# Two transposed score units per exponential in the first attention, and three subtractions moved one slot later

## The chip, the cores and the metric

The kernel runs on one core of one Trainium2 chip. The metric is device time in microseconds (us) of that core for one launch. Its engines run their own instruction lists in order and meet only at semaphores: TensorE (PE, with its weight loads PEld), VectorE (DVE), ScalarE (ACT), GpSimd (POOL) and SyncE (SP, which here only issues DMAs).

## The reference

Two transformer layers over x of 16 batches x 512 rows x 256 columns, each an attention with 16 heads of 16 columns and a feed-forward, all in float32. The change lies in the first attention:

```
qkv = layernorm(x) @ w_qkv + b_qkv
dot = einsum('bhid,bhjd->bhij', q, k)
scores = dot * dot / (|q_i|^2 + |k_j|^2 - 2 * dot + 1e-6)
attn = softmax(scores + causal_mask)
x = x + (attn @ v) @ w_out + b_out
```

## The kernel before

The program has four parts, one after the other: this attention (about the first 1,270 us of the profile), a low-rank feed-forward, a second attention and a second feed-forward. Only the first part is changed, in the function `ratio_attention`.

**Units and slots.** The first attention is cut into 640 units of 128 x 512 scores: 16 batches x 2 halves (8 heads each) x 20 units. Ten units make a group of four heads. A unit holds one block of 512 columns, one of 384 beside one of 128, or two of 256. Every engine walks through the same list of slots n, one unit entering per slot. What each engine does in slot n:

- PE: `dots(n)` (q times k into one of two banks), `turn(n - 6)` (four 128x128 transposes of finished scores into one of two banks, L554), `denoms(n + 3)` (the denominators), then, where the slot has it, preparation of the next half, and `attend` (probabilities times values, L220).
- ACT: `exponential(n - 6)` (L655: exp of the transposed unit, bank to SBUF), `inverse(n + 3)` (L644: Ln of the denominators; after every second one L648: Exp of two units together, 1/denominator), then preparation.
- DVE: `weigh(n)` (L789: dot times 1/denominator), `maxima(n)` (L799: times dot again, and the row maximum), then preparation.
- POOL: `less(n)` and `drop_later(n)` (L921, L930: maximum minus score, masked entries), then preparation.

**Preparation.** During the 20 slots of one half the next half's q, k, norms and values are made. The position in the half is what the texts call "slot 2", "slot 4" and so on (slot 20 is position 0 of the next half). From `PREP_AT`: q at 2, k at 4, the norms at 6, values at 9 and 12 or 13. For q and k: PE projects (L510), ACT stores the leading bf16 part and then the squares (L682, L684), DVE subtracts the leading part from the bank's value (L763, the "rest"), POOL splits the rest in two bf16 parts (L902, L904), SP sends the parts to DRAM and gathers them from there into the stacks that `dots` and `denoms` read. The norms go the same way (PE L520, ACT L691, DVE L769). Only the rest's semaphore, `prep_read`, gives the bank free.

**Banks.** PSUM has 8 banks: 2 for dots, 2 for the transposed scores, 1 for the outputs of `attend`, and 3 shared ones that `denoms`, the preparation and the output steps use in turn, so that each use waits until the use three before it has been read. The projection of k in slot 4 gets the bank of q's projection, and so waits for q's rest; the projection of q in slot 2 gets the bank of `denoms(4)` of slot 1, and so waits for the Ln of that unit.

**Waits that set the order.** `dots(n)` waits until `maxima` of unit n-2 is done; `weigh(n)` waits for `dots(n)` and the inverse; `turn(n)` waits for POOL's unit n and until `exponential(n - 2)` has emptied its bank. `denoms(n + 3)` for the next half begins in slot 17 and there waits until the half's DMA gathers have landed.

## Time and profile before

| | |
|---|---|
| median of 3 runs | 2637.72 us (2631.04 to 2639.08) |
| profiled execution: its own time, its span | 2632.14 us, 2630.4 us |
| mean granted TensorE clock | 0.987 of full speed |
| first to last `exponential` | 52.4 to 1268.4 us |
| 200 to 1200 us: PE, DVE, ACT, POOL busy | 947, 896, 923, 794 us |

The last row is the sum over five stretches of 200 us each. "Busy" is the share of time in which at least one instruction of an engine is in flight; the time between the starts of two neighbouring instructions is shorter than the duration of one, since they overlap.

### The profile page before, as it was taken

How to read it: one execution, taken by the hardware profiler on the slowest of the kernel's cores; microseconds unless marked ns; L12 is line 12 of the kernel's file. 1: busy time of each engine (PE TensorE's matmuls, PEld its weight loads, DVE VectorE, ACT ScalarE, POOL GpSimd, SP SyncE). 2: the span in 40 equal slices, each digit the busy share in tenths (PEclk: the TensorE clock that was granted, in tenths of full speed). 3: DMA queues.
4: the chain of work that ended last, by engine and by line, in shares of the span. 5: the costliest groups of instructions: out<-in, count | busy, mean ns of one | idle time of the engine just before them, and what ended most of it. 6: DMA issues, size and time to landing. Idle time of an engine off the chain costs nothing. (4 is left out here: it accounts for less than half of the span.)

```text
span 2630.4 us, 71983 instructions
## 1 busy us (share of the span) xinstructions
PE 2454.3 (93%) x25252; PEld 1750.0 (67%) x25252; DVE 2083.8 (79%) x6697; ACT 1996.4 (76%) x3679; POOL 1787.9 (68%) x3824
## 2 busy tenths in 40 slices
PE   5999999999999999999879989999999999989998
PEld 3677676667767666777423347767776777668887
DVE  5898898889889889988664578878888888846665
ACT  4999899999999999999524347677677666667776
POOL 4778778778877877887361137777777777756555
PEclk8999999999999999999989999999999999999999
DMA  4344244334334433433100146556655655400011
GB/s 119 65 74 81 55 73 85 72 61 83 72 58 79 85 71 61 77 69 63 37 6 1 37 74 111 99 101 98 106 101 95 105 104 94 64 1 32 25 33 41
DMA packets 110375, 182.00 MB, mean 69 GB/s; under 512 B 27008, under 2 KB 96384, under 8 KB 97920
## 3 DMA queue, kind: packets, MB, share of 16 engines
q1 hardware_dynamic: 106176, 175.82, 35.8%
q8 instruction: 203, 3.33, 0.6%
q10 hardware_dynamic: 3840, 1.58, 0.4%
q14 instruction: 156, 1.28, 0.2%
HBM read 116.25 MB, written 60.29 MB: 67 GB/s over the span
## 5 line engine op out<-in xcount | busy, mean ns | idle before, releaser
L921 POOL TENSOR_SCALAR ratio_scores<-ratio_scores,ratio_max_cols 128x512 f32<-128x512 f32 (+3 forms) x1024 | 539.3, 535 | 169.7 <-DVE ratio_max_cols L799 169.5
L205 PE MATMUL bank<-ratio_k_stack,ratio_q_stack 102*128 102x512 bf16 (+7 forms) x2048 | 508.7, 303 | 42.3 <-DVE ratio_max_cols L799 21.3
L1491 DVE CUSTOM_DVE_ANT_0 zeroed_unused<-bank,zeroed_drop 128x512 bf16<-128x512 f32 (+3 forms) x1024 | 439.7, 485 | 107.4 <-PE bank L205 107.2
L799 DVE CUSTOM_DVE_ANT_0 ratio_scores<-bank,ratio_scores 128x512 f32<-128x512 f32 (+3 forms) x1024 | 472.5, 490 | 22.2
L1373 ACT ACTIVATE arena<-bank 128x512 f32<-128x512 f32 x640 | 370.2, 593 | 151.0 <-PE bank L1266 149.6
L789 DVE TENSOR_TENSOR ratio_scores<-bank,ratio_inverse 128x512 f32<-128x512 f32 x640 | 435.6, 681 | 13.5 <-ACT ratio_inverse L648 6.5
L655 ACT ACTIVATE ratio_prob<-bank 128x512 f32<-128x512 f32 x640 | 378.6, 592 | 81.8 <-PE bank L554 80.9
L644 ACT ACTIVATE ratio_inverse<-bank 128x512 f32<-128x512 f32 x640 | 382.6, 598 | 13.4 <-PE bank L208 13.2
L554 PE MATMUL bank<-const_f_sb,ratio_scores 128*128 128x128 f32 x2560 | 386.5, 273 | 1.2 <-ACT ratio_prob L655 1.0
L648 ACT ACTIVATE ratio_inverse<-ratio_inverse 128x1024 f32<-128x1024 f32 x320 | 338.6, 1058 | 10.1
L1625 POOL TENSOR_SCALAR_AFFINE_SELECT arena<-arena 128x256 f32<-128x256 f32 (+1 forms) x640 | 228.0, 362 | 165.7 <-ACT arena L1373 161.2
L554 PEld LDWEIGHTS bank<-const_f_sb,ratio_scores 128*128 128x128 f32 x2560 | 296.0, 141 | 47.8 <-issue 11.0
L205 PEld LDWEIGHTS bank<-ratio_k_stack,ratio_q_stack 96*128 96x128 bf16 (+1 forms) x2048 | 178.0, 98 | 189.1 <-DVE ratio_max_cols L799 91.5
L930 POOL TENSOR_SCALAR_AFFINE_SELECT ratio_scores<-ratio_scores 128x256 f32<-128x256 f32 (+1 forms) x640 | 230.9, 361 | 47.0
L1266 PE MATMUL bank<-zeroed_q_stack,zeroed_k_stack 99*128 99x128 bf16 x2560 | 249.6, 219 | 11.7 <-ACT arena L1373 10.2
L205 PE MATMUL bank<-zeroed_k_stack,zeroed_q_stack 96*128 96x512 bf16 (+3 forms) x1024 | 247.3, 304 | 3.4 <-PEq L2161 2.1
L1266 PEld LDWEIGHTS bank<-zeroed_q_stack,zeroed_k_stack 99*128 99x128 bf16 x2560 | 178.1, 97 | 91.5 <-ACT arena L1373 55.1
L2414 POOL TENSOR_TENSOR ternary_square_sum<-ternary_square_sum,ternary_squares 128x512 f32<-128x512 f32 x112 | 144.6, 1291 | 121.2 <-ACT ternary_squares L2300 120.8
L208 PE MATMUL bank<-const_b_sb 128*128 128x128 bf16 x1024 | 193.2, 220 | 0.0
L1959 ACT ACTIVATE lowrank_hidden<-bank,lowrank_b 128x512 f32<-128x512 f32 x128 | 82.2, 685 | 132.9 <-PE bank L1841 132.8
L220 PE MATMUL bank<-ratio_prob,ratio_v_ones 128*32 128x128 f32 x5120 | 180.1, 277 | 0.0
L220 PE MATMUL bank<-arena,zeroed_v_ones 128*32 128x128 f32 x5120 | 179.4, 276 | 0.7
(218 smaller groups left out, 4872.0 us busy)
## 6 DMA issues: line engine op xcount, KB each, us to landing
ratio_q_stack<-ratio_parts_q SPq DMA_DIRECT2D x186, 128.0 KB
ratio_k_stack<-ratio_parts_k SPq DMA_DIRECT2D x186, 128.0 KB
zeroed_q_stack<-zeroed_parts_q SPq DMA_DIRECT2D x186, 128.0 KB, 4.5
zeroed_k_stack<-zeroed_parts_k SPq DMA_DIRECT2D x186, 128.0 KB, 7.5
ratio_parts_q<-arena SPq DMA_DIRECT2D x96, 128.0 KB
ratio_parts_k<-arena SPq DMA_DIRECT2D x96, 128.0 KB
zeroed_parts_q<-shared_parts SPq DMA_DIRECT2D x96, 128.0 KB
zeroed_parts_k<-shared_parts SPq DMA_DIRECT2D x96, 128.0 KB
```

What stands on the lines that cost most here:

```text
L205: i = e.matmul(bank[:, off:off + w], qs[0:rows, s, hh, ib * P:(ib + 1) * P], ks[0:rows, s, hh, 0:w], start=(k == 0), stop=mask is None, sk ...
L220: i = e.matmul(o_bank[32 * h:32 * h + 32, ib * P:(ib + 1) * P], values_ones[:, vs, jb, (g % 2) * GROUP + h, :], prob[:, (base + u) % bufs, ...
L554: i = e.transpose(bank[:, at:at + P], scores[:, n % S_BUFS, at:at + P], net.ident)
L644: e.activation(inv[:, n % INV_BUFS, :], shared("denoms", n)[:, :], ACT.Ln, scale=-2.0, bias=EPS_RATIO).then_inc(s["log_den"])
L648: e.activation(both, both, ACT.Exp, scale=-1.0).then_inc(s["inverse"])
L655: e.activation(prob[:, n % PROB_BUFS, 0:wd], exp_banks[n % 2][:, 0:wd], ACT.Exp, scale=-1.0).then_inc(s["prob"])
L789: e.tensor_tensor(scores[:, n % S_BUFS, 0:wd], dot_banks[n % 2][:, 0:wd], inv[:, n % INV_BUFS, 0:wd], ALU.mult).then_inc(s["weighed"])
L799: i = e.tensor_tensor_reduce(seg, dot_banks[n % 2][:, at], seg, 1.0, 0.0, ALU.mult, ALU.max, mx[:, pair % M_BUFS, c:c + 1])
L921: i = e.tensor_scalar(seg, seg, -1.0, mx[:, pair % M_BUFS, c:c + 1], ALU.mult, ALU.add)
L1266: i = e.matmul(bank[:, off + jb * P:off + (jb + 1) * P], ks[0:STACK + FOLD_ROWS, st, hh, jb * P:(jb + 1) * P], qs[0:STACK + FOLD_ROWS, st, ...
L1373: e.activation(prob[:, n % FOLD_PROBS, 0:wd], exp_banks[n % 2][:, 0:wd], ACT.Exp, scale=0.25).then_inc(s["prob"])
L1491: i = e.tensor_tensor_reduce(unused[:, n % 2, at], bank[:, at], drop[:, L - (ib + 1) * P:L], 1.0, 0.0, ALU.add, ALU.max, mx[:, pair % FOLD ...
```

## The change

Three edits:

1. The eight banks become one PSUM tensor of 128 x 8 x 512, so that one ACT instruction can read two neighbouring banks. In every odd slot ACT runs one `exponentials(p)` of 128 x 1024 over the two units n-7 and n-6, and none in even slots. The semaphore `prob` now counts pairs. Probabilities have 14 buffers instead of 13, scores 9 instead of 10.
2. PE transposes units n-7 and n-6 one after the other in odd slots, none in even slots. Both wait until the exponentials of the pair before have emptied both banks.
3. DVE's rests of q and k and of the norms (L763, L769) are issued one slot later, at 3, 5 and 7, behind that slot's `weigh` and `maxima`. PE's, ACT's and POOL's parts of the preparation stay in their slots.

```
-        self.banks = [ctx.enter_context(nc.psum_tensor(f"bank{i}", [P, 512], F32)) for i in range(8)]
+        self.psum = ctx.enter_context(nc.psum_tensor("bank", [P, 8, 512], F32))
+        self.banks = [self.psum[:, i, :] for i in range(8)]
...
-S_BUFS, INV_BUFS, PROB_BUFS = 10, 6, 13
+S_BUFS, INV_BUFS, PROB_BUFS = 9, 6, 14
...
             def turn(n):
...
-                q.wait_ge(s["prob"], n - 1)
+                q.wait_ge(s["prob"], n // 2)
...
-                if 0 <= n - BACK_LAG < total:
+                if 0 <= n - BACK_LAG < total and (n - BACK_LAG) % 2:
+                    turn(n - BACK_LAG - 1)
                     turn(n - BACK_LAG)
...
-                    q.wait_ge(s["prob"], g * N_UNITS + ATTEND_UNITS[part])
+                    q.wait_ge(s["prob"], (g * N_UNITS + ATTEND_UNITS[part] + 1) // 2)
...
-            def exponential(n):
-                wd = width(UNITS[n % N_UNITS])
-                q.wait_ge(s["turned"], n + 1)
-                if n >= PROB_BUFS:
-                    q.wait_ge(s["attended"], attended_by(n - PROB_BUFS))
-                e.activation(prob[:, n % PROB_BUFS, 0:wd], exp_banks[n % 2][:, 0:wd], ACT.Exp, scale=-1.0).then_inc(s["prob"])
+            def exponentials(p):
+                last = 2 * p + 1
+                q.wait_ge(s["turned"], last + 1)
+                if last >= PROB_BUFS:
+                    q.wait_ge(s["attended"], max(attended_by(last - 1 - PROB_BUFS), attended_by(last - PROB_BUFS)))
+                at = 2 * p % PROB_BUFS
+                e.activation(prob[:, at:at + 2, :], net.psum[:, EXP_BANK:EXP_BANK + 2, :], ACT.Exp, scale=-1.0).then_inc(s["prob"])
...
-                if 0 <= n - BACK_LAG < total:
-                    exponential(n - BACK_LAG)
+                if 0 <= n - BACK_LAG < total and (n - BACK_LAG) % 2:
+                    exponentials((n - BACK_LAG) // 2)
...
                 step = ratio_prep_at(n, halves)
-                if step:
+                if step and step[2][0] == "v":
+                    prepare(*step)
+                step = ratio_prep_at(n - 1, halves) if n else None
+                if step and step[2][0] != "v":
                     prepare(*step)
```

What stands in PE's list in slots 4 and 5 of a half (L510 the projection of k, L205 and L208 dots and denominators, L554 transposes, L220 attend), before:

```order
154 L205 MATMUL bank<-ratio_k_stack,ratio_q_stack 128x256 x2
155 L554 MATMUL bank<-const_f_sb,ratio_scores 128x128 x4
156 L205 MATMUL bank<-ratio_k_stack,ratio_q_stack 128x512
157 L208 MATMUL bank<-const_b_sb 128x128
158 L510 MATMUL bank<-arena,ratio_w_in 128x512 x2
159 L205 MATMUL bank<-ratio_k_stack,ratio_q_stack 128x512
160 L554 MATMUL bank<-const_f_sb,ratio_scores 128x128 x4
161 L205 MATMUL bank<-ratio_k_stack,ratio_q_stack 128x384
```

and after, where every line number is one or two higher:

```order
143 L206 MATMUL bank<-ratio_k_stack,ratio_q_stack 128x256 x2
144 L206 MATMUL bank<-ratio_k_stack,ratio_q_stack 128x512
145 L209 MATMUL bank<-const_b_sb 128x128
146 L512 MATMUL bank<-arena,ratio_w_in 128x512 x2
147 L206 MATMUL bank<-ratio_k_stack,ratio_q_stack 128x512
148 L556 MATMUL bank<-const_f_sb,ratio_scores 128x128 x8
149 L206 MATMUL bank<-ratio_k_stack,ratio_q_stack 128x384
```

The four transposes ahead of the projection are gone from slot 4, and eight stand together in slot 5.

DVE's list from `maxima` of slot 2 (the two L799 rows) to slot 5, before; L763 are the rests of q and k:

```order
120 L799 ISA ratio_scores,ratio_max_cols<-bank,ratio_scores 128x512
121 L799 ISA ratio_max_cols 128x1
122 L763 SCALAR_TENSOR_TENSOR arena<-bank,ratio_bias_qk,arena 128x512
123 L789 TENSOR_TENSOR ratio_scores<-bank,ratio_inverse 128x512
...
132 L799 ISA ratio_max_cols 128x1
133 L763 SCALAR_TENSOR_TENSOR arena<-bank,ratio_bias_qk,arena 128x512
134 L789 TENSOR_TENSOR ratio_scores<-bank,ratio_inverse 128x512
```

and after, with L767, L793 and L803 for the three:

```order
120 L803 ISA ratio_scores,ratio_max_cols<-bank,ratio_scores 128x512
121 L803 ISA ratio_max_cols 128x1
122 L793 TENSOR_TENSOR ratio_scores<-bank,ratio_inverse 128x512
...
126 L803 ISA ratio_max_cols 128x1
127 L767 SCALAR_TENSOR_TENSOR arena<-bank,ratio_bias_qk,arena 128x512
128 L793 TENSOR_TENSOR ratio_scores<-bank,ratio_inverse 128x512
```

The rest of q now stands behind slot 3's `weigh` and `maxima`, that of k behind slot 5's.

ACT's list around the end of a half (L655 exponential, L644 Ln, L648 Exp of two), before:

```order
115 L648 ACTIVATE ratio_inverse<-ratio_inverse 128x1024
116 L655 ACTIVATE ratio_prob<-bank 128x512
117 L644 ACTIVATE ratio_inverse<-bank 128x512
118 L655 ACTIVATE ratio_prob<-bank 128x512
119 L644 ACTIVATE ratio_inverse<-bank 128x512
120 L648 ACTIVATE ratio_inverse<-ratio_inverse 128x1024
```

and after (L659, L647, L651):

```order
87 L651 ACTIVATE ratio_inverse<-ratio_inverse 128x1024
88 L659 ACTIVATE ratio_prob<-bank 128x1024
89 L647 ACTIVATE ratio_inverse<-bank 128x512 x2
90 L651 ACTIVATE ratio_inverse<-ratio_inverse 128x1024
```

Of the two exponentials per pair of slots one is left, twice as wide, and it stands where the first one stood, ahead of the Ln of the odd slot.

## Rows read from the trace of the kernel before

**Rows 1.** Page, part 1: busy us, share of the span, instructions.

```profile
PE 2454.3 (93%) x25252; PEld 1750.0 (67%) x25252; DVE 2083.8 (79%) x6697; ACT 1996.4 (76%) x3679; POOL 1787.9 (68%) x3824
```

**Rows 2.** Waits, 200 to 1200 us: us in total, times, longest.

```profile
ACT ratio_prob L655 <- PE bank L554: 66.6, 90, 2.5
DVE arena L763 <- ACT arena L684: 62.1, 51, 2.6
...
DVE ratio_norm_rest L769 <- ACT ratio_n_parts L691: 10.1, 26, 0.6
...
DVE ratio_scores L789 <- PE bank L205: 4.1, 16, 0.8
```

**Rows 3.** Groups of PE, 200 to 1200 us: busy, mean ns | idle before, releasers.

```profile
L205 PE MATMUL bank<-ratio_k_stack,ratio_q_stack 96*128 96x128 bf16 (+5 forms) x1657 | 411.6, 302 | 25.3 <-DVE ratio_max_cols L799 13.7 <-DMA ratio_k_stack<-ratio_norms_k 10.3
...
L510 PE MATMUL bank<-arena,ratio_w_in 128*128 128x512 f32 x208 | 103.2, 618 | 21.8 <-ACT ratio_inverse L644 16.1 <-DVE arena L763 5.3
L532 PE MATMUL bank<-ratio_w_in,arena 128*128 128x128 f32 x416 | 58.2, 283 | 6.1 <-ACT ratio_inverse L644 6.1
```

**Rows 4.** Groups by shape, 400 to 720 us: busy, mean ns.

```profile
L655 ACT ACTIVATE ratio_prob<-bank 128x512 f32<-128x512 f32 x167 | 98.9, 592 | 21.4 <-PE bank L554 21.2
L648 ACT ACTIVATE ratio_inverse<-ratio_inverse 128x1024 f32<-128x1024 f32 x83 | 87.8, 1058 | 2.6
```

**Rows 5.** Timeline, slots 2 to 4 of a half: start, us, engine, line [idle before].

```profile
583.83 1.98 PE L510 MATMUL bank<-arena,ratio_w_in 128*128 128x512 f32 x4 [0.36 <-ACT ratio_inverse L644]
...
585.65 0.38 PE L205 MATMUL bank<-ratio_k_stack,ratio_q_stack 96*128 96x384 bf16 x2
...
585.87 0.60 PE L554 MATMUL bank<-const_f_sb,ratio_scores 128*128 128x128 f32 x4
...
586.31 0.33 PE L205 MATMUL bank<-ratio_k_stack,ratio_q_stack 102*128 102x384 bf16 x1
...
587.15 0.75 DVE L763 SCALAR_TENSOR_TENSOR arena<-bank,ratio_bias_qk,arena 128x512 f32<-128x512 f32 x1 [1.58 <-ACT arena L684]
...
587.82 0.68 DVE L789 TENSOR_TENSOR ratio_scores<-bank,ratio_inverse 128x512 f32<-128x512 f32 x1
...
587.95 1.98 PE L510 MATMUL bank<-arena,ratio_w_in 128*128 128x512 f32 x4 [0.20 <-DVE arena L763]
...
589.23 0.69 DVE L789 TENSOR_TENSOR ratio_scores<-bank,ratio_inverse 128x512 f32<-128x512 f32 x1
```

**Rows 6.** Timeline, slot 10 of the same half: dots(10) on PE, weigh(10) on DVE.

```profile
599.59 0.38 PE L205 MATMUL bank<-ratio_k_stack,ratio_q_stack 96*128 96x512 bf16 x1
...
600.60 0.68 DVE L789 TENSOR_TENSOR ratio_scores<-bank,ratio_inverse 128x512 f32<-128x512 f32 x1
```

**Rows 7.** Timeline, slots 20 to 22 behind an even half, up to the projection of q.

```profile
620.45 0.22 PE L208 MATMUL bank<-const_b_sb 128*128 128x128 bf16 x1
...
620.86 0.59 ACT L644 ACTIVATE ratio_inverse<-bank 128x512 f32<-128x512 f32 x1
...
621.48 1.06 ACT L648 ACTIVATE ratio_inverse<-ratio_inverse 128x1024 f32<-128x1024 f32 x1
...
622.44 0.58 ACT L672 ACTIVATE arena<-bank 128x512 f32<-128x512 f32 x1
...
622.92 0.59 ACT L655 ACTIVATE ratio_prob<-bank 128x512 f32<-128x512 f32 x1
...
623.40 0.60 ACT L644 ACTIVATE ratio_inverse<-bank 128x512 f32<-128x512 f32 x1
...
624.05 1.13 PE L510 MATMUL bank<-arena,ratio_w_in 128*128 128x512 f32 x2 [0.52 <-ACT ratio_inverse L644]
```

**Rows 8.** Timeline of PE and ACT, slots 20 and 21 behind an odd half.

```profile
657.66 0.39 PE L205 MATMUL bank<-ratio_k_stack,ratio_q_stack 96*128 96x384 bf16 x2 [0.25 <-DVE ratio_max_cols L799]
...
659.70 0.59 ACT L644 ACTIVATE ratio_inverse<-bank 128x512 f32<-128x512 f32 x1
...
660.35 1.12 PE L510 MATMUL bank<-arena,ratio_w_in 128*128 128x512 f32 x2
```

**Rows 9.** Timeline of PE and DVE, slots 17 and 18 of an odd half.

```profile
651.36 0.39 PE L205 MATMUL bank<-ratio_k_stack,ratio_q_stack 102*128 102x512 bf16 x1 [0.29 <-DMA ratio_k_stack<-ratio_norms_k]
...
652.75 0.39 PE L205 MATMUL bank<-ratio_k_stack,ratio_q_stack 96*128 96x384 bf16 x2
...
654.72 0.66 DVE L789 TENSOR_TENSOR ratio_scores<-bank,ratio_inverse 128x512 f32<-128x512 f32 x1
```

More of the change, by code:

```diff
@@ L306 @@
 SHARED = 3
+EXP_BANK = 3
 def ratio_prep(b, what):
@@ L460, in ratio_attention @@
         bk = net.banks
-        shared_banks, dot_banks, exp_banks, o_bank = (bk[0], bk[6], bk[7]), bk[1:3], bk[3:5], bk[5]
+        shared_banks, dot_banks, exp_banks, o_bank = (bk[0], bk[6], bk[7]), bk[1:3], bk[EXP_BANK:EXP_BANK + 2], bk[5]
         shared = lambda *use: shared_banks[use_at[use] % SHARED]
```

## The prediction

> **What bounds the kernel now.** I read the page first [rows 1]: PE 93%, DVE 79%, ACT 76%, POOL 68% over the whole program. That says little about one part, so I took the waits between 200 and 1200 us, deep inside the first attention; they cover 26 of its 32 halves. DVE there waits mostly for its own rests: 62.1 us at L763 for ACT's squares and 10.1 us at L769, together 2.8 us per half, and only 4.1 us for dots [rows 2]. ACT waits 66.6 us for transposes. Read alone, this says that DVE is the bound and that its 72 us are to be had. PE's groups over the same stretch speak against it: PE is idle only 25.3 + 21.8 + 6.1 = 53.2 us of 1000, or 2.05 us per half [rows 3]. PE, DVE and ACT are all near their limit and pass the limit on to each other. So I followed the timeline of one half and asked at each step which engine the others wait for. It falls into two stretches.
>
> From the projection of q (slot 2) to dots(10) PE sets the pace. In the half that begins at 583.83 this takes 599.59 - 583.83 = 15.76 us [rows 5, 6], and PE has one gap in it, 0.20 us ahead of k's projection, which waits for q's rest [rows 5]. DVE's waits of 1.58 us and so on lie inside this stretch, and DVE has caught up to one slot behind PE at its end: dots(10) ends at 599.97, weigh(10) starts at 600.60, 0.63 us later [rows 6]. From weigh(10) to the next projection of q DVE sets the pace first, and the last step is ACT's: q's projection waits for the Ln of slot 1, 16.1 us in 26 halves [rows 3].
>
> **Edit 1, ACT: one exponential of two units.** By durations, the wide one costs about what L648 costs, 1058 ns, against 2 x 592: 126 ns less per pair, 40 us of ACT over 320 pairs [rows 4]. But durations overlap. From start to start a 512-wide instruction takes 0.48 us (622.92 to 623.40) and the 1024-wide one 0.96 us (621.48 to 622.44) [rows 7], so two narrow ones cost exactly a wide one and the saving is 0. Bounds: 0 to 126 ns per pair; L648 reads SBUF where the new one reads a bank, so I take near 0, some 0.93 us for the new one from start to start. The Trainium skill ("Perfetto Trace Analysis", Optimizing Scalar/DVE Operations) gives ScalarE a fixed cost of about 51 ns per instruction on PSUM and 93 ns on SBUF, and says that grouping helps where the engine is saturated; by that the saving is an estimated 51 ns per pair, 16 us of ACT time over the kernel. ACT is no bound by itself (it waits 66.6 us for PE), so even 40 us would matter only where its Ln of slot 1 is awaited.
>
> What does move there is the order. Behind an even half ACT is late (it has stored x and kept a row): Ln 620.86, Exp of two 621.48, store of x 622.44, exponential 622.92, Ln 623.40 to 624.00, and PE projects q at 624.05 after 0.52 us idle [rows 7]. After the change the exponential of slot 20 no longer stands ahead, so the first Ln starts when its denominators end, 620.45 + 0.22 = 620.67, say 620.70. Then 0.62 + 0.96 + 0.48 as now gives 622.76, the wide exponential 0.93 more, 623.69, and the Ln 0.60: 624.29. That is **0.29 us later** per such half. Behind an odd half ACT is not late: dots(21) starts at 657.66 [rows 8], two turned units end 0.22 + 2 x 0.44 + 0.16 = 1.26 us later (the steps from dots to transposes and across one unit, 585.65, 585.87, 586.31, and a duration of 0.60) [rows 5], the wide exponential 0.93, the Ln 0.60: 660.45 against 659.70 + 0.59 = 660.29 now [rows 8]. **0.16 us later.** Two narrow exponentials could start after the first unit was turned; one wide one cannot.
>
> **Edit 2, PE: two units turned in odd slots.** PE's work is the same: 0.44 us per unit [rows 5]. I credit nothing for neighbouring transposes. Even slots give up 0.44 us and odd ones take it, so dots(n) of every even slot is issued 0.44 us later where PE is busy, and dots of odd slots as before. It matters where such a dots ends a PE stretch: slot 10. At slots 2, 4 and 6 it takes the transposes out of the slots that hold the projections. The gate from both banks is no wait by itself: the next pair comes two slots later, some 3.8 us, against about 1 us for the exponential. If that cover went, each pair would cost PE the rest of ACT's 0.93 us.
>
> **Edit 3, DVE: rests a slot later.** The wait for squares goes, but k's projection wants q's rest. dots(3) starts 585.65 and ends 586.03; weigh(3) and maxima(3) take 589.23 - 587.82 = 1.41 us, so 587.46; the rest takes 587.82 - 587.15 = 0.67, so 588.13; k's projection starts 0.05 behind it, about 588.20 instead of 587.95 [rows 5]. **0.25 us later**, where today DVE idles 1.58 us for nothing. From there PE is saturated, so dots(10) starts at 599.59 + 0.25 + 0.44 = 600.28 and ends 0.38 later, 600.66; weigh(10) follows at about 600.68 instead of 600.60 [rows 6]. So the 0.69 us fall almost wholly into the 0.63 us that DVE lags today: **0.08 us later** per half. The recovered waits show up as new waits of weigh for dots in slots 5, 6, 7, 8.
>
> POOL's split of q and k stands in its old slot and now waits for the later rest, with `less` of the next unit queued behind it; its results are wanted six slots on, and POOL is busy 68% [rows 1]. k's rest ends about 0.3 us later than now, since DVE arrives there later but does not wait. The gathers land for slot 17, where PE waits 10.3 us in 26 halves [rows 3]. In the odd half shown there the denoms start at 651.36, dots(18) at 652.75, and weigh(18) only at 654.72 [rows 9]: it ends at 653.14, 1.6 us of cover, and two turned units ahead of denoms fill 0.44 us of the wait. I price the DMA path at 0; without that cover it would be 0.3 us in 15 halves, 5 us. Score buffers 9 and probability buffers 14 put their waits behind events at least two slots old: 0.
>
> **Sum.** 31 halves prepare another. Per half with the late ACT 0.29 + 0.08 = 0.37 us, 15 times, 5.6 us; per other half 0.16 + 0.08 = 0.24 us, 16 times, 3.8 us. Together 9.4 us. The profiled execution took 2632.14 us, so 2641.5; it lies 5.6 us under the median of the three runs, and set against that median the forecast is 2637.7 + 9.4 = **2647 us**, 0.36% more. No change can be told from a change within 0.3%, 7.9 us. The likeliest case's own range is 3 to 15 us more, 2641 to 2653.
>
> **Rivals.**
>
> *The rests pay, faster.* If DVE's lag were the real limit at the end of each half, the 2.8 us per half that it waits would come back until PE's idle 2.05 us per half is used up: 31 x 2.05 = 63 us, 2575. Half of it is likelier, since the waits for DMA and for the Ln stay: 32 us, 2606. For it: PE's wait for maxima, 13.7 us [rows 3], and 0.25 us of it just ahead of q's projection [rows 8]. Against: the PE stretch of 15.76 us has no room. It decides if weigh(10) comes over 0.3 us earlier than 16.8 us behind the projection of q, which needs dots(10) to be early. Chance 0.27.
>
> *Nothing moves.* The wide exponential starts to start takes 0.86 us or less, ACT's lateness goes, and merging and shifting cancel within 3 us: 2638. For it: the slacks above are a tenth of a microsecond wide. This is also the case that the wide exponential saves only what the later start costs. Chance 0.14.
>
> *Dots late, and banks held, slower.* Between slots 14 and 20 of an even half PE is full too (output projections). If dots(16) and dots(18) each hold DVE 0.44 us and nothing takes it back, that is 0.88 us in each of 31 halves, 27 us: 2674 with the sum above. Against: in odd halves weigh(18) has 1.6 us of cover [rows 9], and behind even halves the chain through ACT is as long [rows 7]. The Trainium skill ("Perfetto Trace Analysis", Matmuls) wants matmul groups to rotate through PSUM banks so that the evacuation of one overlaps the next group; the change gives that up for the two transposed banks, and, under Optimizing Scalar/DVE Operations of the same page of the Trainium skill, instructions of an engine that isn't saturated are better broken up if they cause bubbles elsewhere. By these rules the time would come out on this side; no row here shows what that costs. It decides once ACT trails PE's odd slot by over two slots less 0.93 us. Chance 0.13.
>
> The forecast has 0.46, of which 0.26 beyond 7.9 us and 0.20 within. Faster: 0.25 (0.02 of that rival is too small to tell). Same: 0.20 + 0.14 + 0.02 = 0.36. Slower: 0.26 + 0.13 = 0.39. For the range I take in the upper half of the faster rival, down to 26 us less, and nearly all of the slower one: 2612 to 2672.
>
> **What would show each step.** Wide exponential: mean near 1.03 to 1.06 us and 0.93 from start to start; if 0.86, edit 1 gives more than I say. L767's wait for ACT gone; in its place about 0.5 us ahead of weigh in slots 5 to 8. Projection of q to projection of k: 4.37 us instead of 4.12. Projection of q to weigh(10): 16.85 instead of 16.77. PE's wait ahead of q's projection for the Ln grows from 0.62 us per half to 0.8. DMA waits in odd halves a little shorter. Two halves, from a projection of q to the second next: 77.1 us instead of 660.35 - 583.83 = 76.5 [rows 5, 8]. I am wrong if q's projection comes no later although the exponential is wide, if dots(10) has slack, or if PE waits for `prob` ahead of the pairs. The other three parts of the program should stay as they are to 1 us.

## The result and the profile after

The changed kernel takes 2660.07 us (median of 4 runs, 2659.28 to 2662.17) against 2637.09 (4 runs, 2631.04 to 2639.08): ratio 1.009, 95% interval 1.0073 to 1.0108. It is 23 us slower, 0.9%, where 0.36% was forecast. The profiled execution has a span of 2657.9 us.

The page of the changed kernel, part 1, and its group of the wide exponential (busy us, mean ns | idle before it):

```profile
PE 2453.8 (92%) x25252; PEld 1750.0 (66%) x25252; DVE 2091.2 (79%) x6697; ACT 1989.9 (75%) x3359; POOL 1789.7 (67%) x3824
...
L659 ACT ACTIVATE ratio_prob<-bank 128x1024 f32<-128x1024 f32 x320 | 325.4, 1017 | 23.3 <-PE bank L556 17.4
```

PE, nearest its limit, and ACT are busy no longer than before; DVE is, by 7.4 us, and POOL by 1.8 [rows 1]. The 23 us are mostly waiting. The waits of the changed kernel between 200 and 1200 us (total, times, longest; its L793, L767, L512, L534, L206, L647, L659 are L789, L763, L510, L532, L205, L644, L655 of before):

```profile
DVE ratio_scores L793 <- PE bank L206: 69.5, 116, 1.7
...
PE bank L512 <- ACT ratio_inverse L647: 22.2, 25, 1.5
PE bank L206 <- DVE ratio_max_cols L803: 17.5, 40, 0.7
...
PE bank L512 <- DVE arena L767: 14.1, 26, 0.5
PE bank L534 <- ACT ratio_inverse L647: 11.8, 13, 0.9
DVE ratio_v_ones L784 <- PE bank L534: 10.9, 26, 0.4
...
PE bank L206 <- DMA ratio_k_stack<-ratio_norms_k: 8.0, 9, 1.3
```

DVE no longer waits for ACT's squares (62.1 us [rows 2]); it waits 69.5 us for dots, where it waited 4.1. PE's own waits, the ones that count, add up to 73.6 us in the five rows of this view, against 51.5 in those of before [rows 3]: 6.1 more for the Ln ahead of q's projection, 8.8 more for q's rest ahead of k's projection, 5.7 more ahead of the values, 3.8 more for the maxima, 2.3 less for DMA.

The timeline of the half that begins at 588.96, from slot 2 to the values in slot 12:

```profile
588.96 1.98 PE L512 MATMUL bank<-arena,ratio_w_in 128*128 128x512 f32 x4 [0.78 <-ACT ratio_inverse L647]
...
591.20 0.69 DVE L793 TENSOR_TENSOR ratio_scores<-bank,ratio_inverse 128x512 f32<-128x512 f32 x1 [0.93 <-PE bank L206]
...
593.42 1.99 PE L512 MATMUL bank<-arena,ratio_w_in 128*128 128x512 f32 x4 [0.54 <-DVE arena L767]
...
602.34 0.69 DVE L793 TENSOR_TENSOR ratio_scores<-bank,ratio_inverse 128x512 f32<-128x512 f32 x1 [0.47 <-PE bank L206]
...
605.68 0.49 DVE L784 TENSOR_TENSOR ratio_v_ones<-bank,ratio_bias_v 128x128 f32<-128x128 f32 x2 [0.42 <-PE bank L534]
...
606.08 0.68 DVE L793 TENSOR_TENSOR ratio_scores<-bank,ratio_inverse 128x512 f32<-128x512 f32 x1
...
609.49 1.16 PE L534 MATMUL bank<-ratio_w_in,arena 128*128 128x128 f32 x8 [0.91 <-ACT ratio_inverse L647]
...
611.78 1.02 ACT L659 ACTIVATE ratio_prob<-bank 128x1024 f32<-128x1024 f32 x1 [0.77 <-PE bank L556]
...
612.70 0.59 ACT L647 ACTIVATE ratio_inverse<-bank 128x512 f32<-128x512 f32 x1
```

k's projection starts 593.42 - 588.96 = 4.46 us behind q's (before 4.12 [rows 5]), weigh(10) 606.08 - 588.96 = 17.12 us (before 16.77 [rows 5, 6]). DVE's last stop before it is new: the values step waits 0.42 us for PE. The wide exponential takes 612.70 - 611.78 = 0.92 us from start to start.

How much a period of two halves has grown is read from the first and the last projection of q behind an even half in the window, 12 periods apart. Before, then after:

```profile
235.44 1.98 PE L510 MATMUL bank<-arena,ratio_w_in 128*128 128x512 f32 x4 [0.52 <-ACT ratio_inverse L644]
...
1162.20 1.98 PE L510 MATMUL bank<-arena,ratio_w_in 128*128 128x512 f32 x4 [0.52 <-ACT ratio_inverse L644]
```

```profile
238.92 1.98 PE L512 MATMUL bank<-arena,ratio_w_in 128*128 128x512 f32 x4 [0.84 <-ACT ratio_inverse L647]
...
1179.64 1.99 PE L512 MATMUL bank<-arena,ratio_w_in 128*128 128x512 f32 x4 [0.84 <-ACT ratio_inverse L647]
```

(1162.20 - 235.44) / 12 = 77.23 us and (1179.64 - 238.92) / 12 = 78.39: 1.16 us more per two halves, 18.6 us over 16 of them. The profiled execution of before lost 1.8 of its 926.8 us in a stretch where the granted clock had fallen to 0.50 (last section); that of the changed kernel has no such stretch there, and with equal clocks the difference is 1.3 us per two halves. The end of the attention adds to it. There PE has little else to do and the gate from both banks, which costs nothing within the halves, is the limit. PE's last transposes in the changed kernel:

```profile
1284.84 1.06 PE L556 MATMUL bank<-const_f_sb,ratio_scores 128*128 128x128 f32 x8 [1.21 <-ACT ratio_prob L659]
1287.11 1.06 PE L556 MATMUL bank<-const_f_sb,ratio_scores 128*128 128x128 f32 x8 [0.77 <-ACT ratio_prob L659]
```

From the last weigh (1263.81 before, 1283.05 after) to the last attend (1270.33 and 1292.41) it is 2.8 us longer. With 0.7 us more up to the first weigh (40.52, 41.22) that makes 22.1 us by which the first attention ends later in the profile; the first weigh comes at 40.4 to 42.8 us in the profiles of all kernels here, so the 0.7 us can be chance. The code behind the first attention is the same in both kernels, and takes 1360.1 us in one profile and 1365.5 in the other (1360.1 to 1368.5 in the 14 profiles of this document). At one place in it the clock differs. The changed kernel, then before:

```profile
2345.00:2350.00 5.00, 4.10 (x11) 3.16 (x12) 0.16 (x1) 0.60 (x1) 0.00 (x0) 0.52 0.00 0
2350.00:2360.00 10.00, 6.06 (x15) 3.68 (x15) 4.11 (x13) 1.36 (x2) 0.76 (x3) 0.50 0.00 0
2360.00:2369.00 9.00, 7.48 (x20) 5.51 (x20) 4.41 (x10) 5.03 (x10) 3.91 (x8) 0.50 0.00 0
```

```profile
2333.00:2336.00 3.00, 2.60 (x6) 2.12 (x7) 2.95 (x8) 1.77 (x2) 2.99 (x9) 0.54 0.00 0
2336.00:2341.00 5.00, 3.28 (x15) 2.35 (x15) 2.18 (x5) 3.40 (x8) 1.70 (x3) 0.94 0.00 0
2341.00:2350.00 9.00, 7.71 (x51) 6.91 (x51) 5.50 (x9) 7.00 (x14) 5.18 (x4) 1.00 0.01 3
```

(The columns are the stretch, its length, busy us and instructions of PE, PEld, DVE, ACT and POOL, the granted clock as a share of 2.4 GHz, the DMA share and GB/s.) The granted clock is 0.50, 1.2 GHz, for some 24 us in the one and 3 us in the other. So the two profiles lie 27.5 us apart and the medians 23, and a difference of 4 or 5 us between medians need not come from the first attention.

### The profile page after: what moved, and what is told of

It is laid out like the page before. It is cut to its first block and busy times, and to the rows that moved or that the text cites. A ratio compares the mean times of both kernels' runs of the same rounds, so it can differ in the third digit from the quotient of the medians.

```text
span 2657.9 us, 71282 instructions
## 1 busy us (share of the span) xinstructions
PE 2453.8 (92%) x25252; PEld 1750.0 (66%) x25252; DVE 2091.2 (79%) x6697; ACT 1989.9 (75%) x3359; POOL 1789.7 (67%) x3824
## 3 DMA queue, kind: packets, MB, share of 16 engines
q14 instruction: 153, 1.25, 0.2%
## 5 line engine op out<-in xcount | busy, mean ns | idle before, releaser
L793 DVE TENSOR_TENSOR ratio_scores<-bank,ratio_inverse 128x512 f32<-128x512 f32 x640 | 437.0, 683 | 102.4 <-PE bank L206 88.8
L206 PE MATMUL bank<-ratio_k_stack,ratio_q_stack 102*128 102x512 bf16 (+7 forms) x2048 | 454.8, 303 | 42.5 <-DVE ratio_max_cols L803 26.5
L803 DVE CUSTOM_DVE_ANT_0 ratio_scores<-bank,ratio_scores 128x512 f32<-128x512 f32 (+3 forms) x1024 | 472.4, 489 | 22.0
L647 ACT ACTIVATE ratio_inverse<-bank 128x512 f32<-128x512 f32 x640 | 371.2, 599 | 80.4 <-PE bank L209 80.3
L651 ACT ACTIVATE ratio_inverse<-ratio_inverse 128x1024 f32<-128x1024 f32 x320 | 338.8, 1059 | 10.1
L659 ACT ACTIVATE ratio_prob<-bank 128x1024 f32<-128x1024 f32 x320 | 325.4, 1017 | 23.3 <-PE bank L556 17.4
L556 PE MATMUL bank<-const_f_sb,ratio_scores 128*128 128x128 f32 x2560 | 332.9, 273 | 4.3 <-ACT ratio_prob L659 4.0
L556 PEld LDWEIGHTS bank<-const_f_sb,ratio_scores 128*128 128x128 f32 x2560 | 287.4, 141 | 32.6 <-issue 13.1
L206 PEld LDWEIGHTS bank<-ratio_k_stack,ratio_q_stack 96*128 96x128 bf16 (+1 forms) x2048 | 178.8, 98 | 192.6 <-issue 81.5
L206 PE MATMUL bank<-zeroed_k_stack,zeroed_q_stack 96*128 96x512 bf16 (+3 forms) x1024 | 246.8, 303 | 3.8 <-PEq L2168 2.1
```

Of the source, the lines that this page charges most:

```text
L206: i = e.matmul(bank[:, off:off + w], qs[0:rows, s, hh, ib * P:(ib + 1) * P], ks[0:rows, s, hh, 0:w], start=(k == 0), stop=mask is None, sk ...
L556: i = e.transpose(bank[:, at:at + P], scores[:, n % S_BUFS, at:at + P], net.ident)
L647: e.activation(inv[:, n % INV_BUFS, :], shared("denoms", n)[:, :], ACT.Ln, scale=-2.0, bias=EPS_RATIO).then_inc(s["log_den"])
L651: e.activation(both, both, ACT.Exp, scale=-1.0).then_inc(s["inverse"])
L659: e.activation(prob[:, at:at + 2, :], net.psum[:, EXP_BANK:EXP_BANK + 2, :], ACT.Exp, scale=-1.0).then_inc(s["prob"])
L793: e.tensor_tensor(scores[:, n % S_BUFS, 0:wd], dot_banks[n % 2][:, 0:wd], inv[:, n % INV_BUFS, 0:wd], ALU.mult).then_inc(s["weighed"])
```

## The experiments

The table gives, from the timelines, means over 13 even and 13 odd halves between 200 and 1200 us, in us: from q's projection to k's; to weigh(10); from weigh(10) to weigh(20), even and odd; from there to the next projection of q, behind even and behind odd; two halves. Behind them the median and its ratio to before. Kernel before as timed beside them: 2637.3 (first four), 2636.6 (next four), 2635.9 (next three), 2637.9 (last). Three rows hold stretches at a granted clock of 0.50 in w10-w20 of odd halves, each behind a long wait of PE for DMA: one in before (1.8 us), two in e1 (4.5 us), five in e5 (12.4 us). The other odd halves take 16.7 us there in all three kernels, except one of 17.22 in e5 and the last, 15.2. Two such stretches lie in q-k of e10 (3.0 us).

```
                    q-k   q-w10  w10-w20 ev/odd  w20-q ev/odd  two halves  median   ratio (95%)
before              4.13  16.77  19.71 / 16.72   3.74 / 3.44   77.15
after               4.46  17.13  20.24 / 16.57   3.57 / 3.69   78.33       2660.1   1.0090 (1.0073-1.0108)
e1_rests_only       4.46  16.70  19.87 / 16.93   3.74 / 3.80   77.75       2647.5   1.0041 (1.0026-1.0056)
e2_pairs_only       4.12  16.79  20.25 / 16.61   3.57 / 3.67   77.67       2648.1   1.0041 (1.0025-1.0057)
e3_values_late      4.46  16.94  20.82 / 17.00   3.57 / 3.58   78.85       2666.4   1.0114 (1.0092-1.0136)
e4_two_narrow       4.46  17.13  20.19 / 16.57   3.63 / 3.52   78.17       2653.2   1.0060 (1.0043-1.0076)
e5_kn_late          4.13  16.37  19.87 / 17.57   3.74 / 3.75   77.67       2639.9   1.0012 (0.9999-1.0024)
e6_rows_even        4.5   17.2   19.52 / 16.57   4.77 / 3.63   78.86       2667.2   1.0107 (1.0092-1.0121)
e7_rests_x_later    4.46  16.70  19.87 / 16.61   3.74 / 3.32   76.95       2632.8   0.9987 (0.9975-0.9999)
e8_before_x_later   4.13  16.77  19.71 / 16.55   3.74 / 3.19   76.74       2629.0   0.9972 (0.9959-0.9985)
e9_kn_late_x_later  4.13  16.37  19.88 / 16.65   3.74 / 3.57   76.57       2627.5   0.9965 (0.9952-0.9978)
e10_rows_early      4.6   17.3   19.89 / 16.58   4.98 / 3.74   79.79       2675.0   1.0148 (1.0131-1.0164)
e11_after_x_later   4.46  17.13  20.24 / 16.57   3.58 / 3.28   77.93       2652.2   1.0060 (1.0044-1.0077)
e12_vb13            4.46  17.13  20.14 / 16.60   3.58 / 3.59   78.16       2656.2   1.0065 (1.0049-1.0081)
```

### e1 and e2: each edit alone

e1 is the kernel before with edit 3 alone; e2 has edits 1 and 2 and DVE's rests where they stood. The core of e1, DVE's loop:

```diff
-                if step:
+                if step and step[2][0] == "v":
+                    prepare(*step)
+                step = ratio_prep_at(n - 1, halves) if n else None
+                if step and step[2][0] != "v":
                     prepare(*step)
```

> The kernel before with edit 3 alone: DVE's rests of q, k and the norms one slot later, transposes and exponentials as before. Theory A (pairing costs, the rests don't): k's projection comes 0.25 to 0.33 us later, but DVE no longer lags at slot 10, so that projection of q to weigh(10) falls from 16.77 to about 16.5 us: 6 to 9 us less than before, 2629 us. Theory B (the later rest of q is what costs): 0.33 us in each of 31 halves, 10 us more than before, 2647 us.

> The changed kernel with DVE's rests back in their old slots: edits 1 and 2 alone. Theory A: most of the 23 us stays; projection of q to weigh(10) is 16.8 us as before, slot 15 of even halves keeps its 0.46 us and q's projection waits for the Ln as in the changed kernel: 13 to 18 us more than before, 2650 to 2655 us. Theory B: the pairs cost little, 10 to 13 us more at most, and k's projection is back at 4.13 us behind q's.

Each costs the same: 10.2 and 10.8 us, together 21 of the 23. So neither pays, and they add. In e1 weigh(10) comes 0.07 us earlier, although k's projection is 0.33 us late: the dots have slack as long as the transposes aren't moved. Its loss is behind weigh(10): 0.16 us in even halves, 0.36 ahead of q's projection behind odd halves, and 0.21 in w10-w20 of odd halves, which is the two stretches at a clock of 0.50. PE's waits in e1, 200 to 1200 us:

```profile
PE bank L205 <- DMA ratio_k_stack<-ratio_norms_k: 16.8, 12, 2.4
PE bank L510 <- DVE arena L763: 14.0, 26, 0.5
```

16.8 us for DMA against 10.3 [rows 3]; that path was priced at nothing. In e2 q to weigh(10) is as before, and the loss is the even half's last ten slots, 0.54 us, and the end of the attention, 2.8 us as in the changed kernel.

### e3 and e4: the values step, and the width

In e3 DVE's values steps too come a slot later than in the changed kernel, so that they don't wait behind the turned pair. In e4 the pair stays but gets two exponentials of 512, the first as soon as the first unit is turned:

```diff
-                q.wait_ge(s["turned"], last + 1)
...
-                e.activation(prob[:, at:at + 2, :], net.psum[:, EXP_BANK:EXP_BANK + 2, :], ACT.Exp, scale=-1.0).then_inc(s["prob"])
+                q.wait_ge(s["turned"], last)
+                e.activation(prob[:, at, :], exp_banks[0][:, :], ACT.Exp, scale=-1.0)
+                q.wait_ge(s["turned"], last + 1)
+                e.activation(prob[:, at + 1, :], exp_banks[1][:, :], ACT.Exp, scale=-1.0).then_inc(s["prob"])
```

> The changed kernel with DVE's step of the values one slot later too (slots 10 and 13 or 14), which the change left in place. The changed trace shows DVE idle 0.42 us there in each half, for PE's values. If that wait lies on the path between the projection of q and weigh(10), that stretch falls from 17.13 to 16.85 us and the kernel is 9 us faster than the changed one, 2651 us. If DVE is late for another reason (dots(10) itself), the wait moves to weigh(10) and the time stays at 2660 us.

> The changed kernel with two 128x512 exponentials in the odd slot instead of the wide one, each behind its own unit's transposes; all else as in the changed kernel. Theory: the wide one saves no time from start to start and can't start before the second unit is turned, so two narrow ones give 0.1 us per pair of halves and more back, 2 to 5 us less than the changed kernel, 2656 us. Rival: one instruction less is worth 0.05 to 0.13 us of ACT per pair ahead of q's projection, and the two narrow ones make it 5 us slower, 2665 us.

e3 splits what weigh(10) lost: 16.94 instead of 17.13, so 0.19 us were the values' wait; the other 0.17 are put down to the late dots(10). But the time rises by 6: behind weigh(10) even halves take 20.82 instead of 20.24 us and odd ones 17.00 instead of 16.57. The step had filled a gap of DVE, and now stands where DVE is full. My forecast missed by 15 us. e4 is 7 us faster than the changed kernel (2653.2 against 2660.1, intervals 1.0043 to 1.0076 and 1.0073 to 1.0108). The table shows 2.6 of them (16 x 0.16), most of it the Ln behind odd halves (3.69 to 3.52), and in its profile the last attend starts 2.8 us earlier (1289.64 against 1292.41) although its first weigh came 0.6 later (41.86). So some 3.4 us are the attention's. The other 4 us lie in the unchanged code behind it, which takes 1361.1 us in this profile against 1365.5, with the granted clock at 0.50 for some 10 us around 2350 instead of 24. The one execution of e4 with a mean clock of 0.983, where the changed kernel's four have 0.983 and 0.984, took 2656.1 us, 4 less than their median. The wide exponential saves nothing, and its later start costs a little.

### e5, e7 and e8: the rests apart, and the load of x

Before, SP issues the load of x (512 KB) right behind the last gather on which the next half's denoms wait. SP's issues in an odd half of before:

```profile
646.59 0.27 SPq L988 DMA_DIRECT2D ratio_k_stack<-ratio_norms_k  x1
646.91 0.40 SPq L1000 DMA_DIRECT2D x<-in_L_attn_x  x1
```

e5 shifts only the rests of k and the norms; e7 (on top of e1) and e8 (on top of before) issue x behind the next half's parts of q:

```diff
-                if m and b + 2 < B:
-                    e.dma_start(net.xb(b + 2), x_dram[b + 2].rearrange("(t p) d -> p t d", p=P)).then_inc(net.x_sems[(b + 2) % X_SEMS], 16)
                 sem = gathered(half)[0]
                 send_parts(half, 0)
+                if m and b + 2 < B:
+                    e.dma_start(net.xb(b + 2), x_dram[b + 2].rearrange("(t p) d -> p t d", p=P)).then_inc(net.x_sems[(b + 2) % X_SEMS], 16)
```

> The kernel before, with only the rests of k and of the norms a slot later; q's and the values' steps stay where they stood. My theory is that moving q's rest alone delays k's projection (4.13 us behind q's before, 4.46 with every rest late), while the steps of k and the norms lie in the stretch that PE sets. So: k's projection back to 4.13 us behind q's, weigh(10) 16.4 to 16.8 us behind q's projection, and 0 to 0.4 us per half less than before: 2625 to 2637 us. The rival is that k's later rest reaches PE by way of the gathers of the odd halves, where the run with all rests late waited 16.8 us for DMA against 10.3: then 3 to 7 us more than before, 2640 to 2644 us. The last group of gathers hangs on k's rest, so if the rival is right PE's wait for DMA between 200 and 1200 us is again above 14 us.

> The kernel before with all rests but the values' a slot later, as in the first experiment (2647.5 us), and in addition the load of x for two batches ahead issued behind the half's own parts, so that it does not share the queues with the gathers of the half before. Theory: the cost of the late rests in the odd halves (PE's wait for DMA 16.8 us between 200 and 1200 us, before 10.3) is a transfer that lands late, and this takes away what it competes with: the wait under 6 us, and 2638 to 2643 us. Rival: the wait is the late issue of the gathers themselves, or only the place where DVE's and PE's lateness shows: 2647 us, with the wait at 16 us as there.

> The kernel before with the load of x issued behind the half's own parts, and nothing else. If the 10.3 us that PE waits for DMA between 200 and 1200 us (11 instances of about 0.9 us, in odd halves) come from the load of x, up to 13 us over the 32 halves go: 2626 to 2634 us. If that wait is hidden or is made by the gathers alone: 2637 us, as before.

e5 confirms both the theory and its rival: weigh(10) gains 0.40 us in every half, the best of all, and the odd halves give it back, where PE waits 19.3 us for DMA in slot 17. What such a wait costs is seen half by half. In odd halves of before, PE's wait in slot 17 and the time from weigh(20) to q's projection, in us:

```
wait           0.29  0.54  0.85  1.09  1.25  1.51
weigh(20)-q    2.83  3.07  3.38  3.62  3.79  4.05
```

With no wait it is 2.79. So nearly the whole wait reaches q's projection, by way of the later denominators and their Ln; beyond some 1.5 us weigh(18) is late too (a half of e5 with a wait of 2.06 us: 17.22 us from weigh(10) to weigh(20) instead of 16.69). Most of the 0.85 us that slots 17 and 18 lose in the table is something else. Five odd halves, behind waits of 1.79 to 2.57 us, take 18.5 to 20.4 us, and in each the granted clock falls to 0.50 right behind the wait, as in this one:

```profile
723.33 0.39 PE L205 MATMUL bank<-ratio_k_stack,ratio_q_stack 102*128 102x512 bf16 x1 [2.43 <-DMA ratio_k_stack<-ratio_norms_k]
...
723.70 1.93 PE L220 MATMUL bank<-ratio_prob,ratio_v_ones 128*32 128x128 f32 x32
```

```profile
720.00:721.00 1.00, 0.89 (x8) 0.57 (x5) 0.96 (x6) 1.00 (x3) 0.93 (x3) 1.00 1.02 117
721.00:723.00 2.00, 0.00 (x0) 0.00 (x0) 1.93 (x7) 1.64 (x3) 0.79 (x2) 1.00 0.99 192
723.00:724.00 1.00, 0.67 (x10) 0.40 (x14) 1.00 (x4) 0.19 (x1) 0.93 (x4) 0.86 0.21 71
724.00:726.00 2.00, 2.00 (x35) 1.34 (x28) 0.58 (x4) 0.41 (x1) 0.82 (x2) 0.50 0.00 0
726.00:727.00 1.00, 1.00 (x7) 0.91 (x6) 0.75 (x2) 0.00 (x0) 0.00 (x0) 0.50 0.00 0
727.00:728.00 1.00, 1.00 (x22) 0.55 (x19) 0.71 (x4) 0.93 (x2) 0.18 (x1) 0.93 0.00 0
```

The five halves are 12.4 us longer together. If the waits cost there what they did at 2.06 us, an estimate from these rows is under 4 us for the waits and over 8 for the clock. How many such stretches the other executions of e5 had is not known; its median is only 3.3 us above before, where the table's 16 x 0.52 would give 8.3.

e8 is faster than before, by 7.6 us (0.9972, 0.9959 to 0.9985), from one moved DMA. The load is issued 20.5 us behind that gather (645.13, 665.63) instead of 0.3. PE's wait for DMA is 5.4 us (before 10.3), no wait in slot 17 is above 1.33 us, and the load lands in 4.6 us instead of 6.4; its line in the DMA issues of before and of e8, 200 to 1200 us:

```profile
x<-in_L_attn_x SPq DMA_DIRECT2D x11, 512.0 KB, 6.4
```

```profile
x<-in_L_attn_x SPq DMA_DIRECT2D x12, 512.0 KB, 4.6
```

Of the 0.41 us per two halves between the two in the table, 0.14 is the stretch at a clock of 0.50 in the profile of before. e7 takes 14.7 us from e1, more than forecast, though PE's wait for DMA is 8.8 us and not under 6. Without the load in the way the late rests cost 3.7 us (2632.8 against 2629.0) and not 10: two thirds of e1's loss are gathers that were issued later and met the load of x, with what the clock then took.

### e9: both gains together

> The kernel before with the rests of k and of the norms a slot later (alone 2639.9 us) and the load of x issued behind the half's own parts (alone 2629.0). In the first of the two, weigh(10) came 16.37 us behind q's projection instead of 16.77 in every half, and slots 17 and 18 of the odd halves gave it back, where PE waited 19.3 us for DMA. Theory: that is the gather in which the load of x shares the queues, and with it moved the gain stays. Even halves then 40.0 us from q to q, odd ones 16.37 + 16.6 + 3.3 = 36.3, together 76.3 against 77.15, 16 times 0.85: 14 us less than before, 2619 to 2627 us, with PE's wait for DMA under 10 us. Rival: the gathers end late for k's own later rest, and the two do not add: 2629 to 2636 us, with the wait still at 12 us or more.

2627.5 us, 8 less than before: the fastest, but not to be told from e8 alone (0.9965, 0.9952 to 0.9978, against 0.9972). The two don't add as hoped. weigh(10) keeps its 0.40 us and slots 17 and 18 lose only 0.1 (16.65 against 16.55), but the next projection of q behind odd halves comes 0.38 us later (3.57 against 3.19). PE still waits 12.5 us for DMA where e8 has 5.4, and by the rows above such a wait ends as one for the Ln. Its waits:

```profile
PE bank L510 <- ACT ratio_inverse L644: 17.8, 23, 1.4
...
PE bank L205 <- DMA ratio_k_stack<-ratio_norms_k: 12.5, 12, 1.8
```

### e11: how much of the changed kernel's loss is DMA

The changed kernel with e7's edit of SP.

> The changed kernel with the load of x issued behind the half's own parts. How much of its 23 us is the DMA path. It waits 8.0 us for DMA between 200 and 1200 us. Theory: its pairs hide part of the late gathers (the wait is less than the 16.8 us with the rests alone), so less is to be had than the 14.7 us which the same edit gave there: 3 to 8 us less than the changed kernel, 2652 to 2657 us. Rival: the cost of the late rests in it is the same DMA wait as without the pairs, then 12 us or more come back, 2645 to 2648.

8 us less, at the edge of the theory's range. Against e8, which has x moved too, it is 23 us slower, as the changed kernel is against before. So within the full change the load of x explains none of the 23 us, although it explains most of what the rests cost alone: the pairs leave the gathers time to land, and take it elsewhere.

### e6, e10 and e12: the even half's last ten slots

Three attempts on the 0.53 us there, each one number in the changed kernel's tables:

```diff
-RATIO_GROUP, RATIO_ROW = BACK_LAG + N_UNITS + 5, (53, 55, 57, 59)
+RATIO_GROUP, RATIO_ROW = BACK_LAG + N_UNITS + 5, (54, 56, 58, 60)      e6
+RATIO_GROUP, RATIO_ROW = BACK_LAG + N_UNITS + 5, (52, 54, 56, 58)      e10
-PREP_AT = ({2: "q", 4: "k", 6: "n", 9: "va", 12: "vb", 16: "x0"},
+PREP_AT = ({2: "q", 4: "k", 6: "n", 9: "va", 13: "vb", 16: "x0"},      e12
```

> The changed kernel, with the steps of the output rows of even halves one slot later, so that they fall in slots without pair transposes. My theory puts about 0.5 us of each even half's loss on slots 13 to 15, where a pair of turned units and a row's projection meet in one slot: then weigh(10) to weigh(20) in even halves falls from 20.24 to about 19.8 us, and the time to 2652 us (16 x 0.5 = 8 us less). The rival is that the place of the rows does not matter, because the pair's own 0.88 us in the odd slot holds DVE there: 20.2 us as now, and 2658 to 2662 us.

> The changed kernel, with the steps of the output rows one slot earlier than in it (slots 12, 14, 16, 18 of even halves instead of 13, 15, 17, 19), again away from the pairs. One slot later, weigh(10) to weigh(20) of even halves fell from 20.24 to 19.52 us, but the fourth step came into slot 0 of the next half and cost 1.5 us there. Theory: the pair and the row's projection in one slot cost the even half about 0.5 us, and with all four steps inside it and apart from the pairs it gets them back: 19.5 to 19.8 us in even halves, odd ones as now, 2650 to 2654 us. Rival: the loss only moves to the slots where the row now stands (dots of even slots ordered behind a row's turn), 20.2 us and 2658 to 2662.

> The changed kernel with the second values step of even halves in slot 13 instead of 12 (where it stands in odd halves). In even halves PE waits for a shared bank ahead of that step until ACT has read a denominator out of it, 11.8 us in 13 even halves between 200 and 1200 us against 6.1 before, 0.44 us more per even half, and weigh(10) to weigh(20) there has grown by 0.53. Theory: this wait is most of the even half's loss, since PE is full up to slot 20 there; one slot later the bank is free, the wait is gone (11.8 us to under 2), weigh(10) to weigh(20) falls from 20.24 to 19.6 to 19.9 us, and the time by 6 to 10 us, to 2650 to 2654. Rival: PE's work is only put into a slot that already holds a pair of turned units and a row's turn, the wait comes up elsewhere and the time stays, 2658 to 2662.

e6 and e10 shorten weigh(10) to weigh(20), by 0.72 and 0.35 us. For e6 that proves nothing, since its fourth step, 0.69 us of DVE behind a wait of 0.71, only went over into the next half. In e10 all four stay inside, so 0.35 us is a gain, and 1.4 us are lost at the border (4.98 against 3.57). There a new wait appears: 8.3 us in 13 halves for ACT's copy of the turned x, which holds one of the three shared banks. The rotation of these banks goes by order, and a moved step hands everybody another bank. e12 takes the wait ahead of the values away (L534 no longer shows in PE's waits). In its place the wait for the maxima is 5.8 us longer (17.5 in the changed kernel) and a new one for the Ln appears:

```profile
PE bank L206 <- DVE ratio_max_cols L803: 23.3, 54, 0.7
...
PE bank L206 <- ACT ratio_inverse L647: 3.7, 13, 0.3
```

The even half gains 0.10 us of the 0.53, the time 4 us (below the rival's range, above the theory's); by the table it is 2.7, and in the profile the last attend comes no earlier (1292.56 against 1292.41), so those 4 us aren't shown to be the attention's. The wait for a shared bank is where the loss shows, and mostly not its cause. With the pairs it is there in e2 too (11.8 us, 6.7 in e1), so it is the pairs that make it; which of their effects, the late dots of even slots or ACT's order, no run separates.

## Why the prediction was right, and where its sizes were off

The time lies in the range, 2612 to 2672, and on the side that had the largest chance, 0.39 against 0.36 and 0.25. It doesn't lie in the likeliest case's own range, 2641 to 2653: the wide one held it because it also covered the rivals. The sum said 9.4 us, 23 were measured, and the trace shows 22 (16 x 1.16, 2.8 and 0.7).

- **Wide exponential, 0.93 us from start to start:** 0.92. Right, and that it gives nothing is shown by e4, whose attention is 3.4 us shorter without it.
- **The Ln ahead of q's projection, 0.62 us per half growing to 0.8:** 22.2 / 26 = 0.85. Right. Over both halves the part behind weigh(10) was forecast at 0.29 + 0.16 = 0.45 us and measured 0.46 (0.53 - 0.15 - 0.17 + 0.25). The sum agrees, the place doesn't: the even half loses 0.53 ahead of slot 20 and gains 0.17 behind it. The -0.15 is the stretch at a clock of 0.50 in the profile of before; without it 0.60 is lost. So 0.45 was partly right by chance. The forecast of 0.16 us behind odd halves is nearly borne out: where PE doesn't wait for DMA, weigh(20) to q's projection takes 3.01 us instead of 2.79.
- **q to k 0.25 us later:** 0.33, and the wait for the rest is 0.54 us.
- **q to weigh(10), "0.08 us later" per half: the step that failed.** It measured 0.36, in 31 halves 11.2 us instead of 2.5. What is put down to the late dots(10) is 0.17 and not 0.08. The other 0.19 was a wait not looked for: the values step of slot 9, which "stays in its slot" on DVE, waits for PE's values, and these now stand behind two turned units. e3 shows the 0.19, and the 0.17 as what is left.
- **DVE's wait for ACT comes back as waits for dots in slots 5 to 8:** right in kind; they begin already in slot 3: 0.93, 0.89, 0.47 and 0.47 us ahead of weigh(3), (5), (6) and (8), 69.5 us in all.
- **The DMA path at 0:** right for the whole change (8.0 us against 10.3), wrong for edit 3 alone (16.8). The 1.6 us of cover hold for weigh(18) only; q's next projection comes later by nearly all of the wait, from some 0.3 us on (2.83 us behind a wait of 0.29, 3.79 behind one of 1.25), so this path was never free. The other cover that the text named was the two turned units ahead of denoms, and without them the late gathers cost 6.5 us (e1's 10.2 less the 3.7 that are left with x out of the way), near the 5 that the text set for that case; part of the 6.5 is the clock.
- **The gate from both banks "no wait by itself":** right within the halves, wrong at the end, where the cover of other PE work is gone. The text had the condition and its price, the rest of ACT's 0.93 us, but not the place. The trace shows 1.21 and 0.77 us ahead of a pair; the end is 2.8 us longer in all. The Trainium skill ("Perfetto Trace Analysis", Matmuls) wants matmul groups to rotate through banks; at the end of the attention the trace agrees with it, and elsewhere nothing of it shows.
- **Rivals.** "The rests pay" is refuted by e1, which is 10 us slower. Yet e5 shows its core: with q's rest left in place weigh(10) comes 0.40 us earlier, above the 0.3 us that the text set as the condition, and the odd halves give it back. "Dots late, and banks held" was the nearer one in kind (between weigh(13) and weigh(16) of even halves, 0.53 us where it had 0.88, and the tail), and odd halves had the cover that the text gave them.

## What to carry to other kernels

Between three engines near their limit an idle wait of one is not a gain to be had: ask of every moved step who waits for what it produces, and list the steps that did *not* move but stand behind the moved ones on another engine, since the unpriced 0.19 us came from there. Before grouping instructions measure their distance from start to start: if two narrow ones cost as much as the wide one, grouping only delays the first result and holds two buffers. Look at what is issued right behind the transfer that somebody waits for; a large load that nobody needs soon, moved 20 us later, gave 7.6 us, where no reordering of the rests or of the pairs gave anything clear of noise. And read a mean half by half before explaining it: most of the 0.85 us here came from five halves of 13, where the clock fell.

## What the runs showed of the hardware

TensorE's granted clock can fall from 1.00 to 0.50 (2.4 to 1.2 GHz) inside a busy stretch and cost over a microsecond at once. Between 100 and 1260 us, deep inside the first attention, the profiles show it once in before, twice in e1, five times in e5 and four times in e10, and never in the changed kernel and the other nine.

In before, e1 and e5 PE had stood idle for DMA in slot 17 of an odd half, 1.74 us in before, 2.16 and 2.40 in e1, 1.79 to 2.57 in e5. The one of before:

```profile
264.19 0.39 PE L205 MATMUL bank<-ratio_k_stack,ratio_q_stack 102*128 102x512 bf16 x1 [1.74 <-DMA ratio_k_stack<-ratio_norms_k]
...
264.57 1.82 PE L220 MATMUL bank<-ratio_prob,ratio_v_ones 128*32 128x128 f32 x32
```

The attend takes 1.82 us instead of 1.08, and the half is 1.8 us longer. Not every such wait is followed by a fall: behind 2.06 us in e5, 1.87 in e2 and 1.82 in e9 there was none.

In e10 PE idled 0.64 us ahead of a dots and 0.95 us ahead of q's projection, and the projection then took 3.65 us instead of 1.98:

```profile
638.00:640.00 2.00, 1.16 (x7) 0.44 (x6) 1.93 (x9) 2.00 (x3) 0.73 (x3) 1.00 0.00 0
640.00:641.00 1.00, 0.24 (x1) 0.24 (x2) 0.96 (x3) 1.00 (x3) 0.93 (x3) 0.87 0.00 0
641.00:642.00 1.00, 1.00 (x2) 0.48 (x3) 0.49 (x2) 0.97 (x2) 0.47 (x2) 0.50 0.00 0
```

The same two gaps stand behind its other even halves too, and only four of those show a fall. None of this made the 23 us, since the profile of the changed kernel has no fall there; before, with one, was 1.8 us slower by it. But one more gap of a microsecond or two can cost another 1.7.
